# Spreading the first chunk's shares from on-chip memory in two expert layers, and one exponential placed earlier

## The chip, the core and the metric

The kernel runs on one core of a Trainium2 chip. The time is device microseconds of one execution. The engines are TensorE (PE, with its weight loads PEld), VectorE (DVE), ScalarE (ACT), GpSimd (POOL) and SyncE (SP), which here only issues DMAs. Sixteen DMA engines carry the transfers.

## What is computed

Two layers over x of 4 x 256 tokens and 256 channels, all float32. Each layer has a gated attention-like part and an expert part, each with a gate from a bidirectional decaying sum (`_bi_wkv`). The change is in the expert parts alone. Layer 0 has 64 experts of 64 channels, of which 6 are chosen per token, and a shared expert; layer 1 has 8 experts of 256 channels, of which 2 are chosen:

```python
# layer 0
h = relu2(jnp.einsum('th,eih->tei', x, w1))      # relu, squared
h = h * w_dense[:, :, None]                      # share of each expert in each token
routed = jnp.einsum('tei,ehi->th', h, w2)
out = routed + relu2(x @ shared_up.T) @ shared_down.T
# layer 1
top_vals, top_idx = jax.lax.top_k(x_flat @ w_router, 2)
w_tok = zeros.at[rows, top_idx].add(softmax(top_vals))
h = square(relu(einsum('nc,ecd->ned', x_flat, w_fc)))
out = einsum('nec,ne->nc', einsum('ned,edc->nec', h, w_proj), w_tok)
```

## The kernel before

Tokens (NT = 1024) lie along the free dimension, channels on the 128 partitions. `moe_phase` is an expert layer, called with `which` 0 and 1. The hidden channels of all experts are cut into chunks of 256 (`NW` = 16 in layer 0, 8 in layer 1; layer 0 has one more ahead for the shared expert, `FIRST` = 1). A chunk has four units: two blocks of 128 hidden channels by two halves of 512 tokens, `u` = 0 to 3, the half running fastest. Each unit goes through these steps:

- PE, `first_layer` (L1790): four matmuls into bank `u`.
- ACT, `unit` (L1673, L1675): relu from the bank into `h2` (ffn_relu), then the square in place.
- POOL (L1662): `hw` (ffn_weighted) = `h2` times the tile `wide` (ffn_wide), which holds each expert's share spread over the partitions of its channels.
- PE, `second` (L1812): four matmuls that add the unit to the result.

PE runs two chunks ahead with its first step: in `turn` each unit's four L1812 matmuls are followed by four L1790 of the chunk after the next. Before the turns PE has done the L1790 of chunks 0 and 1, so it then stands until POOL has weighted the first unit of chunk 0.

The shares are made by DVE from the router's logits (L1718 to L1771), transposed by PE (L1861) and copied by ACT to `wT` (ffn_weights_t, L1701): one expert per partition, 64 partitions in layer 0 and 8 in layer 1, with 1024 tokens of 4 bytes in a row. SP waits for both halves (`wT_ready`), stores `wT` to a DRAM tensor (ffn_shares, L1638), waits for the store, and then calls `follow` for each chunk. `follow` (L1621 to L1633) waits, from chunk 2 on, for POOL to have weighted the chunk before the last, and spreads the rows from DRAM (L1628). In layer 0 a chunk holds four experts: four DMAs, each of one row to 64 partitions, two for each block `t` of 128 channels; POOL waits for block 0's two before unit 0 and for block 1's two before unit 2. In layer 1 a chunk lies within one expert: one DMA of one row to 128 partitions for all four units. Where `more` is set, `follow` also loads a later chunk's weights (L1605, tile feat); in layer 0 that begins with chunk 1 and the load of chunk 4. After chunk 1 layer 0 also issues the loads of the next part's weights (`ahead_of`, L1899 to L1902). All these DMAs go through SP's one queue, in the order in which they are written.

In layer 1 ACT also computes the exponential for the shares (L1696). It waits for `sub_ready` from DVE and stands behind the relu and square of units 0 and 1; DVE waits for it before L1764.

Of the kernel before, what the change touches and what calls it, by code (L numbers as in the profile page):

```python
# [14 lines left out]
P = 128  # L15
B, T, C = 4, 256, 256
CT = C // P
NT = B * T
# [36 lines left out]
def halves(h):  # L55
    return slice(h * HALF, (h + 1) * HALF)
# [1471 lines left out]
def moe_phase(nc, ctx, a, env, which, prior):  # L1528
# [14 lines left out]
    def sb(n, shape, dt=F32):  # L1543
        return ctx.enter_context(nc.sbuf_tensor(name + n, shape, dt))

    def named(n):
        return sem(name + n)

    UNITS, LEAD, SLOTS = 4, 2, 4
    FIRST, NW = NS // 2, NM // 2  # L1550
# [3 lines left out]
    BLOCKS, ROWS = (2, P // PER) if PER < P else (1, 1)  # L1554
# [10 lines left out]
    wide = sb("wide", [P, 2, BLOCKS, NT])  # L1565
    h2, hw = (sb(n, [P, 2, UNITS, HALF]) for n in ("relu2", "weighted"))
# [7 lines left out]
    wT = sb("weights_t", [E, NT])  # L1574
# [9 lines left out]
    wide_in = [[named(f"wide_in{slot}{t}") for t in range(BLOCKS)] for slot in range(2)]  # L1584
# [16 lines left out]
    def known(c):  # L1601
        return isinstance(c, int)

    def load(sp, n, slot):
        sp.dma_start(chunk[:, slot, :, :],  # L1605
                     a[pre + "chunks"][ds(n, 1), :, :, :].rearrange("o p k n -> (o p) k n")).then_inc(chunk_in[slot], 16)
# [13 lines left out]
    def sync(sp, ahead_of=None):  # L1620
        def follow(c, slot, more):  # L1621

            if not known(c) or c >= 2:
                sp.wait_ge(weighted, (c - 1) * UNITS)
            for t in range(BLOCKS):
                for i in range(ROWS):
                    part = slice(i * P // ROWS, (i + 1) * P // ROWS)
                    sp.dma_start(wide[part, slot % 2, t, :],  # L1628
                                 w_dram[ds((c * BLOCKS + t) * ROWS + i, 1), :].rearrange("o n -> (o n)")
                                 .partition_broadcast(P // ROWS)).then_inc(wide_in[slot % 2][t], 16)  # L1630
            if more:
                sp.wait_ge(chunk_done, c - 1 + FIRST)
                load(sp, c + 2 + FIRST, (slot + 2 + FIRST) % SLOTS)  # L1633

        if late:
            late["sync"](sp)
        sp.wait_ge(wT_ready, NH)
        sp.dma_start(w_dram, wT[:]).then_inc(wT_out, 16)  # L1638
        sp.wait_ge(wT_out, 16)
        for c in range(2):  # L1640
            follow(c, c, c + 2 + FIRST >= SLOTS)
        if which == 0:
            ahead_of(sp)
        with sp.Fori(0, (NW - 4) // 4) as k:
            for j in range(2, 6):
                follow(k * 4 + j, j, True)
        for c in range(NW - 2, NW):
            follow(c, c, False)
# [20 lines left out]
    def scalar(act):  # L1669
        def unit(n, j, u, to):  # L1670

            act.wait_ge(hidden_full, n + 1)
            act.activation(h2[:, j, u, :], banks[u][:], ACT.Relu).then_inc(relu_done, 1)  # L1673
            act.wait_ge(relu_done, n + 1)
            act.activation(to[:, j, u, :], h2[:, j, u, :], ACT.Square).then_inc(square_done, 1)  # L1675

        def units(c, j, first=0):
            for u in range(first, UNITS):
                unit(SHARED + c * UNITS + u, j, u, h2)

        if which == 0:
            unit(0, 1, 0, hw)
            act.wait_ge(logits_full, 1)
            act.activation(sc[:], banks[LOGITS][:, 0:TT * E].rearrange("p (t e) -> p t e", t=TT), ACT.Sigmoid)\
               .then_inc(scores_ready, 1)
            for u in range(1, UNITS):
                unit(u, 1, u, hw)
            late["scalar"](act)
            for u in range(UNITS - 1):
                unit(SHARED + u, 0, u, h2)  # L1690
        else:
            act.preload_act_table_set("natural_log_exp_and_others")
            for u in range(2):
                unit(u, 0, u, h2)
            act.wait_ge(sub_ready, 1)
            act.activation(sc[:], sb_[:], ACT.Exp).then_inc(scores_ready, 1)  # L1696
            for u in range(2, UNITS):
                unit(u, 0, u, h2)
        for h in range(NH):
            act.wait_ge(wT_full, h + 1)  # L1700
            act.activation(wT[:, halves(h)], banks[TURNED[h]][0:E, :], ACT.Copy).then_inc(wT_ready, 1)  # L1701
        if which == 0:
            units(0, 0, UNITS - 1)
        units(1, 1)
        if late:
            late["exp"](act, 0)
        with act.Fori(1, NW // 2) as k:
            units(k * 2, 0)
            if late:
                late["exp"](act, k)  # L1710
            units(k * 2 + 1, 1)
# [95 lines left out]
    def tensor(pe):  # L1807
# [66 lines left out]
        for j in range(SLOTS):  # L1874
            turn(NW // SLOTS - 1, j, ahead=j < SLOTS - LEAD, ends=j == SLOTS - 1)

    return dict(sync=sync, tensor=tensor, scalar=scalar, vector=vector, gpsimd=gpsimd, last_sum=last_sum,
                open_sync=open_sync, open_tensor=open_tensor, start=start)

# [278 lines left out]
```

## Time and profile before

| | us |
|---|---|
| median of 3 runs | 1457.3 |
| lowest, highest | 1453.5, 1460.3 |
| profiled execution | 1452.3 |
| its span, first to last instruction | 1450.5 |
| PE busy | 1365.4 (94%) |
| DVE, ACT, POOL busy | 1079.7, 853.9, 462.1 |

Layer 0's expert part runs from about 1018 to 1259 us of the span, that of layer 1 from about 1330 to the end. The profile is of one execution, and every time of day in the rows counts from the span's start. In a timeline, the bracket at the end of a row is the idle time before it and what ended it; rows of the same kind in a row are merged, with their count. The last matmul of a merged row is modelled a little long (1.88 us for four that follow each other every 1.72 us), so distances are better taken from start to start.

### The profile page before, as it was taken

To read this page: it belongs to the slowest core of one execution; us is meant where nothing else is said; L and a number is where in the kernel's file an instruction comes from. 1 tells how busy PE (TensorE), PEld (TensorE's weight loads), DVE (VectorE), ACT (ScalarE), POOL (GpSimd) and SP (SyncE) were. 2 spreads that over 40 slices of the span, in tenths; PEclk is the share of its full clock that TensorE was granted. 3 is DMA by queue.
4 is the path that set the end of the run, shared out by engine and by line. 5 is a ranking of instruction groups with operands and counts; after the bars stand their busy time and mean duration, and the time that the engine had idled before them with its cause. 6 is when DMAs were issued, how large, how long until landed. Compare 5 with 4: busy or idle time off the path is not lost.

```text
span 1450.5 us, 22073 instructions
## 1 busy us (share of the span) xinstructions
PE 1365.4 (94%) x7888; PEld 767.7 (53%) x7888; DVE 1079.7 (74%) x2468; ACT 853.9 (59%) x1745; POOL 462.1 (32%) x375
## 2 busy tenths in 40 slices
PE   0879999999999999999999999988999999999998
PEld 0534754754664574575475476475444444444443
DVE  8898899889789889989988988955599675613000
ACT  4577677678578667767767857755533333212432
POOL 5151161161153135116116115215064343200432
PEclk9999999999999999999999999979999999999999
DMA  3120030030021022003003002102283444100220
GB/s 108 43 94 16 16 124 9 8 116 22 17 76 62 17 66 73 16 16 123 16 2 124 15 17 77 33 17 94 69 232 101 117 128 117 59 0 0 78 97 29
DMA packets 39092, 88.70 MB, mean 61 GB/s; under 512 B 5384, under 2 KB 25352, under 8 KB 37840
## 3 DMA queue, kind: packets, MB, share of 16 engines
q1 hardware_dynamic: 38704, 87.23, 19.5%
q8 instruction: 62, 1.02, 0.3%
q14 instruction: 38, 0.31, 0.1%
q10 hardware_dynamic: 288, 0.14, 0.0%
HBM read 84.77 MB, written 2.59 MB: 60 GB/s over the span
## 4 chain that ended last, share of the span: by engine, by line
PE 68%; DVE 18%; ACT 8%; issue 3%; DMA 2%; POOL 1%; DVEq 0%; ACTq 0%; SPq 0%; POOLq 0%
PE bank L512 13%; PE bank L1812 12%; PE bank L1790 11%; PE bank L1911 5%; DVE m L1179 5%; PE bank L611 4%; PE bank L626 4%; DVE m L1183 3%; PE bank L574 3%; PE bank L541 3%; DVE conv L1082 3%; PE bank L606 2%; PE bank L617 2%; PE bank L628 2%; ACT conv L834 2%
## 5 line engine op out<-in xcount | busy, mean ns | idle before, releaser
L1082 DVE SCALAR_TENSOR_TENSOR conv<-bank,taps,conv 128x510 f32<-128x510 f32 x366 | 270.4, 743 | 27.7 <-ACT conv L820 18.4
L512 PE MATMUL bank<-rT,wf 128*128 128x512 f32 x512 | 253.8, 611 | 6.9 <-DVE conv L1093 4.1
L1662 POOL TENSOR_TENSOR ffn_weighted<-ffn_relu,ffn_wide 128x512 f32<-128x512 f32 x96 | 128.7, 1374 | 299.9 <-DMA ffn_wide<-ffn_shares 148.0
L1812 PE MATMUL bank<-ffn_weighted,feat 128*128 128x512 f32 x400 | 186.8, 595 | 3.8 <-POOL ffn_weighted L1662 3.8
L1790 PE MATMUL bank<-rT,feat 128*128 128x512 f32 x400 | 187.4, 595 | 0.0
L1325 POOL TENSOR_TENSOR sq<-sq,qsq 128x512 f32<-128x512 f32 x64 | 82.9, 1296 | 270.3 <-ACT sq L1008 269.6
L1673 ACT ACTIVATE ffn_relu<-bank 128x512 f32<-128x512 f32 x100 | 59.6, 596 | 182.3 <-PE bank L1790 182.3
L512 PEld LDWEIGHTS bank<-rT,wf 128*128 128x128 f32 x512 | 89.5, 191 | 87.9 <-issue 73.7
L1812 PEld LDWEIGHTS bank<-ffn_weighted,feat 128*128 128x128 f32 x400 | 76.0, 190 | 100.1 <-issue 98.2
L1790 PEld LDWEIGHTS bank<-rT,feat 128*128 128x128 f32 x400 | 76.0, 191 | 93.9 <-issue 93.1
L574 PE MATMUL bank<-rT,wz 128*128 128x512 f32 x256 | 115.3, 604 | 8.9 <-DVE m L1183 6.1
L549 PE MATMUL bank<-zs,wo 128*128 128x512 f32 x256 | 119.9, 595 | 3.0 <-DVE m L1183 3.0
L820 ACT ACTIVATE conv<-bank,taps 128x512 f32<-128x512 f32 x122 | 84.1, 712 | 47.2 <-PE bank L512 46.7
L1427 DVE TENSOR_TENSOR xT<-xT,bank 128x512 f32<-128x512 f32 x16 | 10.6, 685 | 130.4 <-PE bank L1812 112.7
L1330 POOL TENSOR_TENSOR zs<-zs,rs 128x512 f32<-128x512 f32 x64 | 81.7, 1277 | 62.4 <-DVE rs L1119 61.7
L1372 POOL COPY t<-tmp 32x1024 f32<-32x1024 f32 x16 | 16.5, 1030 | 265.3 <-DVE tmp L1239 264.8
L1209 DVE TENSOR_TENSOR tmp<-mt,rs 128x126 f32<-128x126 f32 (+35 forms) x488 | 99.3, 243 | 1.2 <-DVE mt L1200 0.5
L1343 POOL TENSOR_TENSOR z<-z,mask 128x512 f32<-128x512 f32 x64 | 81.1, 1277 | 43.0 <-DMA z<-decay_rows 41.3
L1179 DVE SCALAR_TENSOR_TENSOR m<-bank,ccol,z 128x512 f32<-128x512 f32 x128 | 94.6, 739 | 0.2
L574 PEld LDWEIGHTS bank<-rT,wz 128*128 128x128 f32 x256 | 48.7, 193 | 74.0 <-issue 62.7
L626 PE MATMUL bank<-m,z 128*128 128x256 f32 x256 | 77.8, 386 | 2.6 <-DVE rs L1119 2.5
L865 ACT ACTIVATE z<-z,gcol 128x256 f32<-128x256 f32 x128 | 63.4, 495 | 23.4 <-POOL z L1343 23.2
(235 smaller groups left out, 2612.0 us busy)
## 6 DMA issues: line engine op xcount, KB each, us to landing
z<-decay_rows SPq DMA_DIRECT2D x64, 384.0 KB, 4.0
ffn_wide<-ffn_shares SPq DMA_DIRECT2D x64, 256.0 KB, 5.3
feat<-in_L_chunks_dram SPq DMA_DIRECT2D x25, 512.0 KB, 4.2
wf<-in_wf_dram SPq DMA_DIRECT2D x8, 1024.0 KB, 4.9
wz<-in_wz_dram SPq DMA_DIRECT2D x8, 512.0 KB, 3.6
wo<-in_wo_dram SPq DMA_DIRECT2D x8, 512.0 KB, 3.8
ffn_wide<-ffn_shares SPq DMA_DIRECT2D x8, 512.0 KB, 4.0
m<-in_fT_dram SPq DMA_DIRECT2D x2, 512.0 KB, 5.1
```

The costliest lines, as they stand in the source:

```text
L512: ins = pe.matmul(banks[bank_of(p, n)][:], wf[:, c, ORDER[n // NH], :], rT[:, c, halves(n % NH)], start=(c == 0), stop=(c == CT - 1))
L549: ins = pe.matmul(banks[b][:], wo[:, v, c * P:(c + 1) * P], zs[:, v, halves(h)], start=(v == 0), stop=(v == GV - 1))
L574: last = pe.matmul(banks[n % 4][:], wz[:, c, v, :], rT[:, c, halves(h)], start=(c == 0), stop=(c == CT - 1))
L626: pe.matmul(b[:, i * T:(i + 1) * T], z[:, v, 2 * s, :], m[:, v * B + s, 0:T], start=True, stop=False, skip_group_check=True)
L820: act.activation(conv[:, n % HF, :], banks[bank_of(p, n)][:], ACT.Copy, scale=taps[:, ORDER[n // NH], KS - 1:KS]).then_inc(conv0_ready, 1)
L1082: dve.scalar_tensor_tensor(acc[:, :, k:], src[:, :, 0:T - k], taps[:, ORDER[n // NH], KS - 1 - k:KS - k], acc[:, :, k:], ALU.mult, ALU.add ...
L1179: dve.scalar_tensor_tensor(to[:, 0:2 * T].rearrange("p (a i) -> p a i", a=2), banks[b0][:].rearrange("p (a i) -> p a i", a=2), ccol[:, v, ...
L1209: return t, dve.tensor_tensor(t, mt[:, j, rows].unsqueeze(2).to_broadcast([P, n, j + 1]), inv[:, j, 0:j + 1].unsqueeze(1).to_broadcast([P, ...
L1325: pool.tensor_tensor(out, out, qsq[:, n // 4, halves(n % NH)], ALU.add).then_inc(sum_ready, 1)
L1662: pool.tensor_tensor(hw[:, j, u, :], h2[:, j, u, :], wide[:, j, u // NH % BLOCKS, halves(u % NH)], ALU.mult).then_inc(weighted, 1)
L1790: last = pe.matmul(banks[u][:], chunk[:, slot, c, t * P:(t + 1) * P], rT[:, c, halves(h)], start=(c == 0), stop=(c == CT - 1))
L1812: last = pe.matmul(banks[4 + 2 * c + h][:], chunk[:, slot, CT + t, c * P:(c + 1) * P], of, start=start, stop=stop, skip_group_check=True)
```

## The change

For chunk 0 alone, `follow` takes the row from `wT` in SBUF and not from the DRAM tensor, and SP issues these DMAs ahead of the store of `wT` and of its wait. Chunk 1 and all later ones still read DRAM; their first issue stands behind the store's wait as before. In layer 1 the exponential of ACT stands ahead of the relu and square of unit 1.

```diff
@@ follow, in sync
                 for i in range(ROWS):
                     part = slice(i * P // ROWS, (i + 1) * P // ROWS)
+                    if known(c) and c == 0:
+                        row = t * ROWS + i
+                        sp.dma_start(wide[part, slot % 2, t, :], wT[row:row + 1, :].unsqueeze(1).to_broadcast([1, P // ROWS, NT]))\
+                          .then_inc(wide_in[slot % 2][t], 16)
+                        continue
                     sp.dma_start(wide[part, slot % 2, t, :],
                                  w_dram[ds((c * BLOCKS + t) * ROWS + i, 1), :].rearrange("o n -> (o n)")
                                  .partition_broadcast(P // ROWS)).then_inc(wide_in[slot % 2][t], 16)
@@ sync
         sp.wait_ge(wT_ready, NH)
+        follow(0, 0, 2 + FIRST >= SLOTS)
         sp.dma_start(w_dram, wT[:]).then_inc(wT_out, 16)
         sp.wait_ge(wT_out, 16)
-        for c in range(2):
-            follow(c, c, c + 2 + FIRST >= SLOTS)
+        follow(1, 1, 3 + FIRST >= SLOTS)
@@ scalar, layer 1
-            for u in range(2):
-                unit(u, 0, u, h2)
+            unit(0, 0, 0, h2)
             act.wait_ge(sub_ready, 1)
             act.activation(sc[:], sb_[:], ACT.Exp).then_inc(scores_ready, 1)
-            for u in range(2, UNITS):
+            for u in range(1, UNITS):
                 unit(u, 0, u, h2)
```

SP's queue in layer 0, from the transposed shares to the mixer's first weights. First before, then after (a name on the left of the arrow is written, those on the right are read; ffn0_shares is the DRAM tensor, ffn0_weights_t the tile `wT`):

```order
76 L1638 DMA ffn0_shares<-ffn0_weights_t 64x1024
77 L1628 DMA ffn0_wide<-ffn0_shares 64x1024 x8
78 L1605 DMA feat<-in_L0_chunks_dram 128x1024
79 L1899 DMA mixer_win<-in_mixer_in_dram 128x2x1024
80 L1900 DMA mixer_wconv<-in_mixer_conv_dram 128x4x512
```

```order
76 L1630 DMA ffn0_wide<-ffn0_weights_t 64x1x1024 x4
77 L1644 DMA ffn0_shares<-ffn0_weights_t 64x1024
78 L1633 DMA ffn0_wide<-ffn0_shares 64x1024 x4
79 L1605 DMA feat<-in_L0_chunks_dram 128x1024
80 L1903 DMA mixer_win<-in_mixer_in_dram 128x2x1024
```

Four of the eight spreads have moved ahead of the store and read ffn0_weights_t; everything else keeps its place. (The line numbers of the changed kernel are higher by 4 or more.) In layer 1 the same happens to the first of its spreads.

ScalarE's order in layer 1, from unit 0's relu (ffn1_relu2 is `h2`, ffn1_scores takes the exponential). Before, then after:

```order
1005 L1673 ACTIVATE ffn1_relu2<-bank 128x512
1006 L1675 ACTIVATE ffn1_relu2<-ffn1_relu2 128x512
1007 L1673 ACTIVATE ffn1_relu2<-bank 128x512
1008 L1675 ACTIVATE ffn1_relu2<-ffn1_relu2 128x512
1009 L1696 ACTIVATE ffn1_scores<-ffn1_biased 128x64
```

```order
1005 L1678 ACTIVATE ffn1_relu2<-bank 128x512
1006 L1680 ACTIVATE ffn1_relu2<-ffn1_relu2 128x512
1007 L1700 ACTIVATE ffn1_scores<-ffn1_biased 128x64
1008 L1678 ACTIVATE ffn1_relu2<-bank 128x512
1009 L1680 ACTIVATE ffn1_relu2<-ffn1_relu2 128x512
```

The exponential has moved ahead of unit 1's two steps.

## Rows read from the trace of the kernel before

**Rows 1.** The page: span, and the busy time of TensorE.

```profile
span 1450.5 us, 22073 instructions
...
PE 1365.4 (94%) x7888; PEld 767.7 (53%) x7888; DVE 1079.7 (74%) x2468; ACT 853.9 (59%) x1745; POOL 462.1 (32%) x375
```

**Rows 2.** The chain that ended last, layer 0: start us, us, what.

```profile
1042.18 0.97 ACT ffn_weights_t L1701 x2
...
1043.17 2.98 DMA ffn_shares<-ffn_weights_t
...
1046.74 4.08 DMA ffn_wide<-ffn_shares
```

**Rows 3.** The same chain, layer 1.

```profile
1343.00 1.78 DMA ffn_shares<-ffn_weights_t
...
1344.80 3.92 DMA ffn_wide<-ffn_shares
```

**Rows 4.** Timeline of PE, layer 0: start us, us, engine, line, instruction.

```profile
1041.67 8.75 PE L1790 MATMUL bank<-rT,feat 128*128 128x512 f32 x20
...
1052.36 2.90 PE L1812 MATMUL bank<-ffn_weighted,feat 128*128 128x512 f32 x4 [1.94 <-POOL ffn_weighted L1662]
1055.06 2.67 PE L1790 MATMUL bank<-rT,feat 128*128 128x512 f32 x4
1057.56 1.88 PE L1812 MATMUL bank<-ffn_weighted,feat 128*128 128x512 f32 x4
...
1061.00 1.88 PE L1812 MATMUL bank<-ffn_weighted,feat 128*128 128x512 f32 x4
```

**Rows 5.** Timeline of PE, layer 1.

```profile
1340.52 1.04 PE L1861 MATMUL bank<-ident,ffn_weights 128*8 128x128 f32 x8
...
1350.26 1.96 PE L1812 MATMUL bank<-ffn_weighted,feat 128*128 128x512 f32 x4 [1.83 <-POOL ffn_weighted L1662]
1352.05 1.88 PE L1790 MATMUL bank<-rT,feat 128*128 128x512 f32 x4
```

**Rows 6.** Stretches; last three columns: granted clock, share of 16 DMA engines, GB/s.

```profile
1446.40:1447.20 0.80, 0.23 (x1) 0.00 (x0) 0.53 (x1) 0.00 (x0) 0.00 (x0) 1.00 0.88 330
1346.50:1348.50 2.00, 1.92 (x5) 0.57 (x3) 0.00 (x0) 1.27 (x3) 0.00 (x0) 1.00 0.80 299
1044.30:1045.80 1.50, 1.50 (x5) 0.71 (x4) 0.00 (x0) 1.04 (x2) 0.00 (x0) 1.00 0.81 175
65.40:66.30 0.90, 0.90 (x10) 0.90 (x10) 0.86 (x2) 0.00 (x0) 0.00 (x0) 1.00 0.85 179
1343.70:1344.40 0.70, 0.70 (x4) 0.22 (x3) 0.00 (x0) 0.67 (x2) 0.00 (x0) 1.00 0.33 47
1048.00:1052.00 4.00, 2.42 (x6) 0.76 (x4) 0.00 (x0) 3.02 (x6) 1.05 (x1) 1.00 1.03 245
...
1052.00:1056.00 4.00, 3.64 (x6) 1.57 (x7) 3.45 (x3) 0.45 (x1) 4.00 (x4) 0.65 1.05 238
```

**Rows 7.** Timeline of POOL, the first units of layer 0 and of layer 1.

```profile
1050.95 12.01 POOL L1662 TENSOR_TENSOR ffn_weighted<-ffn_relu,ffn_wide 128x512 f32<-128x512 f32 x8 [43.26 <-DMA ffn_wide<-ffn_shares]
...
1348.85 9.84 POOL L1662 TENSOR_TENSOR ffn_weighted<-ffn_relu,ffn_wide 128x512 f32<-128x512 f32 x8 [98.44 <-DMA ffn_wide<-ffn_shares]
```

**Rows 8.** Timeline of PE at its first work in the span.

```profile
37.33 3.65 PE L295 MATMUL bank<-pT,rT 128*128 128x64 f32 x16 [37.33 <-DVE rT L238]
40.77 4.70 PE L512 MATMUL bank<-rT,wf 128*128 128x512 f32 x8
...
49.38 1.89 PE L295 MATMUL bank<-pT,rT 128*128 128x64 f32 x16
```

**Rows 9.** Timeline of SP's queue, layer 0.

```profile
1043.17 0.55 SPq L1638 DMA_DIRECT2D ffn_shares<-ffn_weights_t  x1
1046.17 5.00 SPq L1628 DMA_DIRECT2D ffn_wide<-ffn_shares  x8
1051.21 0.58 SPq L1605 DMA_DIRECT2D feat<-in_L_chunks_dram  x1
```

**Rows 10.** Timeline of ACT and DVE in layer 1, around the exponential.

```profile
1336.73 0.23 DVE L1755 TENSOR_TENSOR ffn_biased<-ffn_masked,ffn_top 128x64 f32<-128x64 f32 x1
...
1337.28 0.60 ACT L1673 ACTIVATE ffn_relu<-bank 128x512 f32<-128x512 f32 x1 [2.24 <-PE bank L1790]
...
1338.45 0.24 ACT L1696 ACTIVATE ffn_scores<-ffn_biased 128x64 f32<-128x64 f32 x1
...
1338.80 0.23 DVE L1764 SCALAR_TENSOR_TENSOR ffn_weights<-ffn_marked,ffn_scores 128x64 f32<-128x64 f32 x1 [0.41 <-ACT ffn_scores L1696]
...
1339.55 0.23 DVE L1771 TENSOR_TENSOR ffn_weights<-ffn_weights,ffn_total 128x64 f32<-128x64 f32 x1
```

**Rows 11.** DMAs from issue to landing (last column): the page, then 1065 to 1070 us.

```profile
feat<-in_L_chunks_dram SPq DMA_DIRECT2D x25, 512.0 KB, 4.2
...
feat<-in_L_chunks_dram SPq DMA_DIRECT2D x1, 512.0 KB, 7.2
```

## The prediction

> **What bounds the kernel now.** The page says that TensorE (PE) is busy for 94% of the span, so time is won or lost only where PE stands still [rows 1]. The change lies in the two expert layers, so I read the chain that ended last around the start of each. In both it leaves PE at the same place: two matmul groups end, ScalarE copies the transposed shares to SBUF, SP stores them to DRAM, SP spreads the first chunk's rows from DRAM over the partitions, GpSimd multiplies, and PE goes on [rows 2, 3]. The store costs 2.98 us in layer 0 and 1.78 us in layer 1; the first spread lands 4.08 and 3.92 us after its issue. PE's own timeline says what of this is seen: PE stands still for 1.94 us before 1052.36 in layer 0 and for 1.83 us before 1350.26 in layer 1 [rows 4, 5]. In layer 0 the two groups behind the gap also take 2.70 and 2.50 us from start to start where the next ones take 1.72, a loss of 1.76 us, and the stretch from 1052 to 1056 shows a granted clock of 0.65, that is a time at 1.2 instead of 2.4 GHz; layer 1 shows no such loss [rows 4 to 6]. All that this change could give back is 1.94 + 1.76 + 1.83 = 5.5 us, 0.38% of the time.
>
> **What it moves on SP.** The first chunk's spreads (four DMAs in layer 0, one in layer 1) now go out when the store did, at 1043.17 and 1343.00, and the store follows them. If a spread from SBUF moved like one from DRAM, everything would be there 3.0 and 1.8 us earlier and both gaps would close. The whole question is how fast 16 DMA engines can read one row: the row of an expert lies in one partition (0 to 3 in layer 0, 0 in layer 1), and it is read 64 times, or 128 times, from there.
>
> **What a DMA from few partitions costs.** No row shows this very transfer, so I bound it by the neighbours. The columns are the share of 16 engines and GB/s; their quotient is the rate of one engine while it is busy [rows 6]. The output store, from 128 partitions: 330/(0.88 x 16) = 23.4 GB/s. A spread to 128 partitions from DRAM: 299/(0.80 x 16) = 23.4. The store of the shares in layer 0, from 64 partitions: 175/(0.81 x 16) = 13.5. The store of the decay rows, from 32 partitions: 179/(0.85 x 16) = 13.2. The store of the shares in layer 1, from 8 partitions: 47/(0.33 x 16) = 8.9. Two stores that both end in DRAM differ by 1.7, so DRAM's side isn't what halves the rate; where fewer partitions are read, an engine gets less. The spreads of layer 0 show the same on the writing side, 245/(1.03 x 16) = 14.9 with 64 partitions each against 23.4 with 128. I read this as paths into SBUF that engines share, two to a path where half the partitions take part, each path passing 2 x 13.5 = 27.0 GB/s. One partition then has one path, whatever the number of engines. I take 27.0 GB/s, since it is the rate of a path that is shared, as it would be here; 23.4, that of one engine alone on it, is the slow bound; the other bound is that there is no such limit and the spreads gain 5.5 us (first rival).
>
> The Trainium skill has a rule that speaks against this change: SBUF — State Buffer, section "Door 1: The DMA port swizzle (why `[64,N]` ≈ `[32,N]`)", says that partitions 0 to 3 all lie on one of sixteen ports, and that a transfer over them reached 27.6 GB/s. By that figure the transfers below would take 38.0 and 19.0 us instead of 38.8 and 19.4 us, and the sum would be an estimated 1.2 us smaller. The stores from 64 and from 32 partitions agree with its claim that these two are alike (13.5 and 13.2 GB/s).
>
> **Layer 0.** A chunk is four DMAs of 64 x 4096 B, 1.049 MB in all, so 38.8 us at 27.0 GB/s, and 19.4 us for the first two. The store took 2.98 us, of which 1.2 us is its movement (0.262 MB at 216 GB/s), so 1.8 us stand beside the movement. First half lands at 1043.17 + 1.8 + 19.4 = 1064.4, all four at 1083.8. From landing to GpSimd's start it was 0.13 us (1050.82 to 1050.95 [rows 2, 7]), from there to PE 1.41 us. (Layer 1: 0.12 and 1.41 [rows 3, 5, 7].) Units 0 and 1 need the first half: PE starts again at 1065.9 instead of 1052.36 and runs out at about 1075 (two units of 3.44 us, plus a slow restart). Unit 2 needs the second half: PE starts it at 1083.8 + 1.54 = 1085.3 instead of 1061.00 [rows 4]. That is **+24.3 us**, and it contains the gain of the store's 3.0 us. A second restart comes on top. Its nearest rows are at the span's start, where PE comes from 37 us of rest: 16 small matmuls take 3.65 us against 1.89 us later, 8 large ones 4.70 us against 2 x 1.88 [rows 4, 8], a loss of 2.7 us. The near bound is layer 1's gap, with none. I take **+2.7**, the rest being nearer to the long one.
>
> What comes behind: the store is issued at about 1045.7 but queues behind the spreads and lands near 1085.0. Only then does SP issue chunk 1's spreads, the weight load of chunk 4 and the mixer's weights; eight spreads took 5.00 us to issue, so four take 2.5 [rows 9]. Chunk 1's first half lands near 1091; PE wants it at 1085.3 + 2 x 3.44 + 2.7 = 1094.9, GpSimd 1.4 us earlier. That leaves some 2 us. The load of chunk 4, issued at 1088 and wanted by PE at 1094.9, has 7 us; one such load took 4.2 us in the median and 7.2 us where it followed four spreads [rows 11]. I count 0, with 0 to 3 as bounds.
>
> **Layer 1.** One DMA of 128 x 4096 B from partition 0: 0.524 MB, 19.4 us, landing at 1343.00 + 1.8 + 19.4 = 1364.2; PE starts at 1365.7 instead of 1350.26, **+15.5**, and a slow restart after 17 us of rest, **+2.7**. It feeds all four units, so there is no second wait. Chunk 1's spread is issued about 1 us after that landing and PE has 13.7 us until it needs it.
>
> **The exponential.** In layer 1 it starts at 1338.45, behind unit 1's square; its input is there at 1336.96. Moving it ahead ends VectorE's wait of 0.41 us. Behind that stand the transposes on PE, but PE reaches them at 1340.52 straight out of its own matmuls, 0.74 us after VectorE's last product at 1339.78 [rows 5, 10]. ScalarE's copy then waits for unit 3's relu and square, which PE's end releases. The relu of unit 1 is due at 1337.28 and the exponential takes 0.24 us from about 1337.0. So it is worth **0**, and PE's own matmuls are what covers it.
>
> **Sum.** 24.3 + 2.7 + 15.5 + 2.7 = 45.2 us. The profiled execution took 1452.3 us (span 1450.5, 1.8 around it), so 1497.5 on its scale. The median of the three runs is 1457.3, 5 us above it, so I forecast **1502.5 us** for a median.
>
> **Rivals.** *No shared path (not slower).* Sixteen engines read one row as fast as they read 128 partitions. Then GpSimd starts 3.0 us earlier in layer 0, at 1047.95, and its product is there at 1049.4, before PE's last matmul of that run ends at 1050.42; in layer 1 1.8 of the 1.83 us go. Gain 5.5 us, 1451.8. It decides from the point where the first half lands by 1048.9, which asks for over 130 GB/s out of one partition pair; the rows with 8 partitions speak against it. Also possible is part of it, a path limit of 40 to 60 GB/s, with some 10 to 30 us lost, 1467 to 1487.
> *A single partition is slower than a path.* All rows have at least 8 partitions. At half the rate (13.5 GB/s) the halves land at 1083.8 and 1122.6 and layer 1 at 1383.6: 24.3 + 38.8 + 15.5 + 19.4 + 5.4 = 103 us, 1561.
> *Engines, not paths.* A DMA whose source is one partition might be given to a single engine. At 23.4 GB/s that engine needs 1.049/23.4 = 44.8 us and 22.4 us: 9.0 us more than the sum, 1511. The time hardly tells it apart, the records do: packets of 0.17 us on one engine rather than some 2.4 us on sixteen.
> The Trainium skill, DMA: Bandwidth & Descriptors, section "Why a DMA increments its semaphore by 16 and not by 1", has the slowest dimension that isn't 1 choose the number of engines, and that is 64 or 128 here. By that page the DMA spreads over sixteen engines.
>
> **Chances.** Serial reading at 23 to 28 GB/s, by paths or by one engine: 0.79. Half of that rate: 0.06. Part of the limit: 0.05. No limit: 0.10. Within the first, the bounds are 45.2 - 5.4 (no slow restarts) = 40 us and 45.2 + 9.0 + 3 = 57 us, so 1497 to 1514; three runs of the kernel before spread over 7 us, which makes it 1493 to 1518, and I reach a little into the partial case: 1484 to 1522. A measurement of this kernel can tell about 0.5% from no change. Slower by more than that: 0.89, within it: 0.09, faster: 0.02, since even the full gain is 0.38%.
>
> **What would show it.** GpSimd's first product at about 1064.5 and 1364.3 instead of 1050.95 and 1348.85, its third at about 1084; PE idle for some 15, 10 and 17 us; a DMA share near 1 at some 27 GB/s while the spreads run; SP's store issued by 1046 and landing after 1084. Wrong would be a first product before 1055, GB/s in the hundreds in these stretches, or a wait on chunk 4's weights of over 3 us.

## The result, and the profile after

The changed kernel takes 1496.7 us (median of 6 runs, 1496.2 to 1503.4) against 1458.2 us (6 runs): 1.028 times the time of before, interval 1.026 to 1.031. It is slower, by 38.5 us between the medians. The profiled execution took 1496.4 us with a span of 1494.6, 44.1 us more than the profiled one of before.

TensorE's timeline has the loss in three gaps. Columns: start, duration, engine, line, instruction, and in brackets the idle time before it and what ended it. Layer 0, to be read against [rows 4]:

```profile
1041.07 8.75 PE L1794 MATMUL bank<-rT,feat 128*128 128x512 f32 x20
1065.58 3.75 PE L1816 MATMUL bank<-ffn_weighted,feat 128*128 128x512 f32 x4 [15.76 <-POOL ffn_weighted L1667]
...
1084.23 3.78 PE L1816 MATMUL bank<-ffn_weighted,feat 128*128 128x512 f32 x4 [9.65 <-POOL ffn_weighted L1667]
1087.81 2.92 PE L1794 MATMUL bank<-rT,feat 128*128 128x512 f32 x4
1090.56 1.88 PE L1816 MATMUL bank<-ffn_weighted,feat 128*128 128x512 f32 x4
```

Layer 1, against [rows 5]:

```profile
1391.68 3.75 PE L1816 MATMUL bank<-ffn_weighted,feat 128*128 128x512 f32 x4 [17.12 <-POOL ffn_weighted L1667]
1395.22 2.81 PE L1794 MATMUL bank<-rT,feat 128*128 128x512 f32 x4
1397.87 1.88 PE L1816 MATMUL bank<-ffn_weighted,feat 128*128 128x512 f32 x4
```

The gaps of 1.94 and 1.83 us have become 15.76 + 9.65 and 17.12 us. Who was late says POOL's timeline, against [rows 7]: it waited for the spreads, twice in layer 0, since units 0 and 1 need two of them and unit 2 the other two.

```profile
1064.17 2.94 POOL L1667 TENSOR_TENSOR ffn_weighted<-ffn_relu,ffn_wide 128x512 f32<-128x512 f32 x2 [57.11 <-DMA ffn_wide<-ffn_weights_t]
1082.91 2.48 POOL L1667 TENSOR_TENSOR ffn_weighted<-ffn_relu,ffn_wide 128x512 f32<-128x512 f32 x2 [15.80 <-DMA ffn_wide<-ffn_weights_t]
...
1390.27 9.82 POOL L1667 TENSOR_TENSOR ffn_weighted<-ffn_relu,ffn_wide 128x512 f32<-128x512 f32 x8 [113.73 <-DMA ffn_wide<-ffn_weights_t]
```

What the DMA engines did meanwhile, by stretches as in [rows 6] (last three columns: granted clock, share of 16 engines, GB/s), and the landings (last column: median us from issue):

```profile
1045.00:1055.00 10.00, 4.82 (x12) 1.84 (x10) 3.05 (x6) 5.36 (x9) 0.00 (x0) 0.87 0.91 26
1370.00:1388.00 18.00, 4.56 (x11) 1.71 (x9) 0.00 (x0) 4.37 (x8) 0.00 (x0) 0.68 0.99 29
```

```profile
ffn_wide<-ffn_weights_t SPq DMA_DIRECT2D x4, 256.0 KB, 25.4
ffn_wide<-ffn_weights_t SPq DMA_DIRECT2D x1, 512.0 KB, 21.0
```

Nearly all sixteen engines are busy, and together they move 26 to 29 GB/s, where spreads from DRAM moved 245 and 299. So they are occupied without moving much. Whether they stand in one line for one path, as I had forecast, is what the probes below test.

SP's queue shows the one thing that came out differently, against [rows 9]:

```profile
1042.56 17.47 SPq L1630 DMA_DIRECT2D ffn_wide<-ffn_weights_t  x4
1060.07 9.59 SPq L1644 DMA_DIRECT2D ffn_shares<-ffn_weights_t  x1
1083.94 2.42 SPq L1633 DMA_DIRECT2D ffn_wide<-ffn_shares  x4
```

Issuing four DMAs took 17.5 us instead of 2.5, and the store behind them 9.6 us. One by one, the first two took 0.54 and 0.60 us, the third 6.61 and the fourth 9.59. In layer 1, where a single spread stands ahead of the store, SP issued both in 0.53 us each (1369.14 and 1369.72), though that spread was as slow.

### The profile page after: what moved, and what is told of

Same layout as the page of the kernel before. It is cut to its first block, busy times and chain, and to the rows that moved or that the text cites. A ratio compares the mean times of both kernels' runs of the same rounds, so it can differ in the third digit from the quotient of the medians.

```text
span 1494.6 us, 22073 instructions
## 1 busy us (share of the span) xinstructions
PE 1371.6 (92%) x7888; PEld 769.9 (52%) x7888; DVE 1069.2 (72%) x2468; ACT 856.1 (57%) x1745; POOL 459.2 (31%) x375
## 4 chain that ended last, share of the span: by engine, by line
PE 66%; DVE 18%; ACT 7%; issue 4%; DMA 3%; POOL 1%; DVEq 0%; ACTq 0%; SPq 0%; POOLq 0%
PE bank L512 13%; PE bank L1816 11%; PE bank L1794 10%; DVE m L1179 5%; PE bank L1915 5%; PE bank L611 4%; PE bank L626 3%; DVE m L1183 3%; PE bank L574 3%; DMA ffn_wide<-ffn_weights_t 3%; PE bank L541 3%; DVE conv L1082 3%; PE bank L606 2%; PE bank L617 2%; ACT conv L834 2%
## 5 line engine op out<-in xcount | busy, mean ns | idle before, releaser
L1082 DVE SCALAR_TENSOR_TENSOR conv<-bank,taps,conv 128x510 f32<-128x510 f32 x366 | 270.5, 743 | 27.7 <-ACT conv L820 18.3
L1816 PE MATMUL bank<-ffn_weighted,feat 128*128 128x512 f32 x400 | 191.3, 607 | 42.5 <-POOL ffn_weighted L1667 42.5
L1209 DVE TENSOR_TENSOR tmp<-mt,rs 128x126 f32<-128x126 f32 (+35 forms) x488 | 102.7, 257 | 1.2 <-DVE mt L1200 0.5
```

The lines of the kernel that those rows point to most:

```text
L1082: dve.scalar_tensor_tensor(acc[:, :, k:], src[:, :, 0:T - k], taps[:, ORDER[n // NH], KS - 1 - k:KS - k], acc[:, :, k:], ALU.mult, ALU.add ...
L1209: return t, dve.tensor_tensor(t, mt[:, j, rows].unsqueeze(2).to_broadcast([P, n, j + 1]), inv[:, j, 0:j + 1].unsqueeze(1).to_broadcast([P, ...
L1816: last = pe.matmul(banks[4 + 2 * c + h][:], chunk[:, slot, CT + t, c * P:(c + 1) * P], of, start=start, stop=stop, skip_group_check=True)
```

## Experiments

"The changed kernel" is the one above; ratios are to the kernel before, measured on the same chip.

### One row, many rows, and pairs of rows

```python
one(0, 64)     # rows[0:1, :] repeated to 64 partitions; then to 128, then to the upper 64
rows[0:64, :]  # 64 partitions to 64; then 128 to 128, 32 to 32
# then pairs of one(0, 64) from SP and one(r, 64) from ACT, with r = 1, 32, 64, 4
```

> Only transfers, nothing of the reference is computed. One row of 4096 B is copied inside SBUF: from partition 0 to 64 partitions, to 128, and to the upper 64; then 64, 32 and 128 partitions each to itself elsewhere; then one DRAM row to 64 and to 128 partitions; then four pairs of one-row copies at the same time from two queues, where the second row lies in partition 1, 32, 64 or 4 beside partition 0. My theory (a path into SBUF of some 27 GB/s that several partitions share): one row to 64 lands after 1.8 + 9.5 = 11 us, to 128 after 21 us; 64 partitions to 64 after 3.0 us, 128 to 128 after 3.5 us; in the pairs with partitions 1 and 32 both need 20 us, with 64 and 4 both are done after 11 us. Rival 1 (a single partition is the limit, not a path): all four pairs are done after 11 us. Rival 2 (a row read over and over is slow for each engine, wherever it lies): all four pairs need 20 us. Rival 3 (any DMA from SBUF to SBUF is slow): 64 to 64 needs 11 us too.

Measured, from issue to landing (last column; to_one is the single row, to_all many rows, to_dram one row out of DRAM):

```profile
to_one<-rows SPq DMA_DIRECT2D x1, 512.0 KB, 20.7
to_all<-rows SPq DMA_DIRECT2D x1, 512.0 KB, 2.9
to_dram<-rows_dram SPq DMA_DIRECT2D x1, 512.0 KB, 3.4
...
to_one<-rows SPq DMA_DIRECT2D x1, 256.0 KB, 11.1
to_all<-rows SPq DMA_DIRECT2D x1, 256.0 KB, 2.9
```

The same bytes, the same number of partitions written, the same queue: 20.7 us out of one partition, 2.9 us out of 128, 3.4 us out of one row of DRAM. So neither SBUF to SBUF (rival 3) nor the repetition as such is slow; a repeated row out of DRAM took 0.5 us more than 128 rows out of SBUF. The first two cases came in as expected to within 0.3 us. The pairs were a poor design. In all four one copy landed long before the other:

```profile
to_same_port<-rows ACTq DMA_DIRECT2D x1, 256.0 KB, 20.7
to_same_port<-rows SPq DMA_DIRECT2D x1, 256.0 KB, 11.8
...
to_other_port<-rows SPq DMA_DIRECT2D x1, 256.0 KB, 11.0
to_other_port<-rows ACTq DMA_DIRECT2D x1, 256.0 KB, 18.3
```

In each, one queue's copy landed after 11 to 12 us, nearly as if alone, and the other's 7 to 9 us later. I read this as one copy after the other, the engines mostly on one row and then on the next. Two copies in turn need some 20 us by the theory and by rivals 1 and 2 alike, so the pairs say little. They were not quite alike: with partition 1 or 32 beside 0 the later copy needed 20.7 us, with 64 or 4 it needed 18.7 and 18.3, and over the first 9 us the pairs moved 27 and 31 GB/s. That goes the way of the theory, but it is far smaller than the 20 against 11 us that I had asked for.

### Sets of partitions

```python
src = rows[lo:hi:by, :]      # n partitions (rows[lo:hi, :] where by is 1), each row read eight times, into DRAM
sp.dma_start(to[name], src.unsqueeze(1).to_broadcast([n, 8, NT]))
```

> Only transfers, nothing of the reference is computed. In the first probe the paired copies went one after the other, so it couldn't tell a shared path from a row that is slow for every engine. Here one DMA at a time reads n partitions, each row of 4096 B eight times, into DRAM. An engine reads one partition's row, and the sets differ in which partitions they hold: 0,1,2,3; 0,4,8,12; 0,32,64,96; 0 to 7; 0,4,..,28; 0 to 15; 0,4,..,60; 0,8,..,120; and last partition 0 alone. The Trainium skill (SBUF — State Buffer, section Door 1) maps partitions to ports by groups of four, with p and p+32 on one port. By that map and 27 GB/s a port, 0-1-2-3 needs 131 kB over one port, 4.9 us, and 0-4-8-12 over four ports 1.3 us; 0-32-64-96 over two ports 2.5 us; 0 to 7 over two ports 9.8 us; 0,4,..,28 over eight ports 1.3 us; 0 to 15 over four ports 5.0 us, 0,4,..,60 and 0,8,..,120 over eight ports 2.5 us; each plus 1.8 us beside the movement. Shared path (my theory, without saying which partitions share): sets with the same number of partitions differ strongly. Rival 1 (the single partition is the limit): each engine has a partition of its own, so all sets move at an engine's full rate, 1.3 us. Rival 2 (a row that is read again and again is slow wherever it lies): all sets of four are equally slow.

One stretch inside each case's movement, in the order of the expectation without the last (columns: stretch, length, POOL busy, clock, share of 16 engines, GB/s):

```profile
6.20:10.80 4.60, 0.00 (x0) 1.00 0.21 23
12.90:14.10 1.20, 0.00 (x0) 1.00 0.14 58
15.80:18.10 2.30, 0.00 (x0) 1.00 0.20 41
20.20:24.80 4.60, 0.00 (x0) 1.00 0.41 45
26.90:28.00 1.10, 0.00 (x0) 1.00 0.29 119
29.80:34.60 4.80, 0.00 (x0) 1.00 0.83 90
36.60:39.00 2.40, 0.00 (x0) 1.00 0.67 149
40.80:43.20 2.40, 0.00 (x0) 1.00 0.70 149
```

GB/s over (share x 16) is the rate of one busy engine:

| partitions read | GB/s of one engine | engines to a port, by the map |
|---|---|---|
| 0, 1, 2, 3 | 6.8 | 4 |
| 0, 4, 8, 12 | 25.9 | 1 |
| 0, 32, 64, 96 | 12.8 | 2 |
| 0 to 7 | 6.9 | 4 |
| 0, 4, .., 28 | 25.6 | 1 |
| 0 to 15 | 6.8 | 4 |
| 0, 4, .., 60 | 13.9 | 2 |
| 0, 8, .., 120 | 13.3 | 2 |

The rate follows the last column alone, at about 27 GB/s for a port, whatever the number of partitions or the number of engines. Rival 1 (each partition has its own 27 GB/s) asked for 26 in every row; rival 2 (a repeated row is slow) asked for the same low rate in the first three. Both fall. (The last case, partition 0 alone, holds 32 KB, too little for a rate that means much; between 44.5 and 45.8 it moved 25 GB/s.) The port map of the Trainium skill (SBUF — State Buffer, "Door 1") agrees with every row, including 0, 32, 64, 96, where it puts p and p + 32 on one port. One number of my expectation was a slip: 262 kB over two ports is 4.9 us and not 9.8; the row's 6.9 GB/s is what two ports give.

### The same place in the queue, many partitions

```diff
-sp.dma_start(wide[part, slot % 2, t, :], wT[row:row + 1, :].unsqueeze(1).to_broadcast([1, P // ROWS, NT]))
+sp.dma_start(wide[part, slot % 2, t, :], wT[:] if which == 0 else rT[:, 0, :])
 # ... .then_inc as before
```

> The changed kernel, but the first chunk's spreads read as many partitions as they write: the 64 rows of the transposed shares in layer 0, and 128 partitions of another tile in layer 1. So the first chunk is weighted with wrong shares; bytes, queue places, waits and everything else are those of the change. Theory (shared paths into the partitions that are read): the first half lands 3 to 4.5 us after 1042.6, TensorE's gaps of 15.8, 9.7 and 17.1 us are gone, and the time falls below the kernel before by up to 5.5 us: ratio 0.996 to 1.000, 45 us less than the changed kernel. Rival (reading from SBUF ahead of the store costs it by queue order or by SBUF-to-SBUF as such): it stays near the changed kernel, ratio 1.02 to 1.03.

Ratio 0.994 (0.993 to 0.996), 1447.5 us. TensorE's timeline has no idle time left ahead of the weighted matmuls, in layer 0 (at 1049.89) or in layer 1 (at 1344.02):

```profile
1041.30 8.75 PE L1794 MATMUL bank<-rT,feat 128*128 128x512 f32 x20
1049.89 1.88 PE L1816 MATMUL bank<-ffn_weighted,feat 128*128 128x512 f32 x4
1051.60 1.88 PE L1794 MATMUL bank<-rT,feat 128*128 128x512 f32 x4
...
1337.15 7.03 PE L1794 MATMUL bank<-rT,feat 128*128 128x512 f32 x16
1344.02 1.88 PE L1816 MATMUL bank<-ffn_weighted,feat 128*128 128x512 f32 x4
```

The order, the waits and the bytes are those of the change; only the source differs (many rows once each in place of one row repeated, so the shares of chunk 0 are not the right ones). With that the kernel is 49 us faster than the changed one, and SP issues its four DMAs in 3.2 us. This is the first rival of the prediction, built on purpose. It gains more than I had put as its ceiling: 10 us between the medians, 6.3 us between the profiled executions (1452.3 and 1446.0), against 5.5. The ratio also lies below the 0.996 to 1.000 that I had expected.

### Layer 1 alone, and the exponential alone

```diff
 # layer 1 alone: in layer 0 the store and its wait stand first again
-                    if known(c) and c == 0:
+                    if which == 1 and known(c) and c == 0:
 # ...
-        follow(0, 0, 2 + FIRST >= SLOTS)
+        if which == 1:
+            follow(0, 0, 2 + FIRST >= SLOTS)
         sp.dma_start(w_dram, wT[:]).then_inc(wT_out, 16)
         sp.wait_ge(wT_out, 16)
+        if which == 0:
+            follow(0, 0, 2 + FIRST >= SLOTS)
```

> The change without its part in layer 0: there the store and the spreads from DRAM stand as before. Theory: the losses of the two layers are separate and add up. Layer 1 cost 15.3 us of waiting and 2.75 us of slow restart, so 18.0 us over the kernel before, ratio 1.0125. Rival: the delay in layer 0 shifts something that layer 1 needs (or the other way), and layer 1 alone costs clearly less than 16 or more than 20 us.

Ratio 1.012 (1.010 to 1.014), 1474.6 us, so 17.2 us over before, of 38.5 for both. The wait in layer 1 is the same as in the changed kernel, the slow stretch behind it is not:

```profile
1371.13 3.57 PE L1819 MATMUL bank<-ffn_weighted,feat 128*128 128x512 f32 x4 [17.15 <-POOL ffn_weighted L1670]
1374.54 1.88 PE L1797 MATMUL bank<-rT,feat 128*128 128x512 f32 x4
1376.25 1.88 PE L1819 MATMUL bank<-ffn_weighted,feat 128*128 128x512 f32 x4
```

The two groups take 3.41 and 1.71 us from start to start, a loss of 1.7 us, where the changed kernel lost 2.75 behind a gap of the same length. The 17.2 us lie within the 16 to 20 that separate layers asked for. Layer 0 alone was not run, so that the layers add up rests on the profile: the changed kernel's layer 0 costs 23.8 + 2.9 us and its layer 1 15.3 + 2.7, and these make the 44.1 us between the spans to within 0.6.

```diff
 # the exponential alone, in the kernel before
-            for u in range(2):
-                unit(u, 0, u, h2)
+            unit(0, 0, 0, h2)
             act.wait_ge(sub_ready, 1)
             act.activation(sc[:], sb_[:], ACT.Exp).then_inc(scores_ready, 1)
-            for u in range(2, UNITS):
+            for u in range(1, UNITS):
```

> The kernel before with the exponential of layer 1 ahead of unit 1's relu, and nothing else. Theory: 0 us, ratio 0.998 to 1.002; VectorE's wait of 0.41 us before its first product with the scores goes, its last product ends 0.3 to 0.4 us earlier, and TensorE's transposes still start straight out of its own matmuls. Rival: the exponential delays unit 1's relu or the transposes follow it, and the gap of 1.83 us before layer 1's first weighted matmul changes by over 0.2 us.

Ratio 0.999 (0.996 to 1.001), 1454.2 us: no change that can be measured. VectorE's product with the scores has no wait before it any more, its last one ends 1.1 us before the transposes (0.74 before), and the transposes still start where TensorE's own matmuls end:

```profile
1342.25 0.23 DVE L1763 SCALAR_TENSOR_TENSOR ffn_weights<-ffn_marked,ffn_scores 128x64 f32<-128x64 f32 x1
...
1343.00 0.23 DVE L1770 TENSOR_TENSOR ffn_weights<-ffn_weights,ffn_total 128x64 f32<-128x64 f32 x1
...
1344.34 1.04 PE L1860 MATMUL bank<-ident,ffn_weights 128*8 128x128 f32 x8
...
1354.19 3.03 PE L1811 MATMUL bank<-ffn_weighted,feat 128*128 128x512 f32 x4 [1.95 <-POOL ffn_weighted L1662]
1357.02 2.54 PE L1789 MATMUL bank<-rT,feat 128*128 128x512 f32 x4
```

The last two rows tell something else. Behind the gap of layer 1, which is hardly longer than before (1.95 against 1.83 us), the two groups take 2.83 and 2.38 us from start to start instead of 1.79 and 1.72, 1.7 us lost, which the profile of before did not have there [rows 5].

### Shortening the gap: few rows first, or TensorE as the spreader

The kernel before pays for a store of all rows and a wait. Chunk 0 needs only 4 rows of 64, or 1 of 8.

```diff
-        sp.dma_start(w_dram, wT[:]).then_inc(wT_out, 16)
-        sp.wait_ge(wT_out, 16)
-        for c in range(2):
-            follow(c, c, c + 2 + FIRST >= SLOTS)
+        now = BLOCKS * ROWS
+        sp.dma_start(w_dram[0:now, :], wT[0:now, :]).then_inc(wT_out, 16)
+        sp.wait_ge(wT_out, 16)
+        follow(0, 0, 2 + FIRST >= SLOTS)
+        sp.dma_start(w_dram[now:, :], wT[now:, :]).then_inc(wT_out, 16)
+        sp.wait_ge(wT_out, 32)
+        follow(1, 1, 3 + FIRST >= SLOTS)
```

> The kernel before, but SP first stores only the rows that chunk 0 needs (4 in layer 0, 1 in layer 1), waits, spreads them from DRAM, and stores the rest behind. Theory: the store's landing falls from 2.98 us to about 1.8 us in layer 0 (the time that 8 rows took in layer 1) and stays 1.7 to 1.8 us in layer 1. TensorE's gap in layer 0 shrinks by 1.2 us, and part of the 1.8 to 2.9 us lost to the lower clock behind it may go; 1.2 to 3 us in all, ratio 0.998 to 0.999 against a resolution of some 0.2%. Rival (the store's time is nearly all latency): the gap stays within 0.3 us.

Ratio 0.995 (0.993 to 0.997), 1448.9 us: faster than both kernels by more than the noise, and more than the 0.998 to 0.999 that I had expected. The waits behind the small stores are 1.76 and 1.24 us (SP goes on at 1044.92 and 1341.43), the gaps shrink to 0.82 and 1.03 us, and no slow group follows either of them:

```profile
1043.16 0.34 SPq L1639 DMA_DIRECT2D ffn_shares<-ffn_weights_t  x1
1044.92 2.46 SPq L1628 DMA_DIRECT2D ffn_wide<-ffn_shares  x4
...
1051.24 1.95 PE L1815 MATMUL bank<-ffn_weighted,feat 128*128 128x512 f32 x4 [0.82 <-POOL ffn_weighted L1665]
1053.03 1.88 PE L1793 MATMUL bank<-rT,feat 128*128 128x512 f32 x4
...
1340.19 0.26 SPq L1639 DMA_DIRECT2D ffn_shares<-ffn_weights_t  x1
1341.43 0.32 SPq L1628 DMA_DIRECT2D ffn_wide<-ffn_shares  x1
...
1346.64 1.96 PE L1815 MATMUL bank<-ffn_weighted,feat 128*128 128x512 f32 x4 [1.03 <-POOL ffn_weighted L1665]
```

Between the profiled executions: 1.12 + 1.76 us in layer 0 and 0.80 us in layer 1, 3.7 us, and the spans differ by 3.6 (1450.5 and 1446.9). The medians differ by 9.0. In layer 1 I had expected no gain; a store of one row landed 0.5 us sooner than one of eight.

The other way has no transfer at all for the first two units (for layer 1: for all four). Before its transposes TensorE multiplies one expert's column, repeated as stationary operand, by the identity:

```python
col = w[:, h * TT // NH + t, i:i + 1].to_broadcast([P, P // ROWS])
last = pe.matmul(banks[SPREAD[h]][i * P // ROWS:(i + 1) * P // ROWS, t * P:(t + 1) * P], col, ident[:], start=True, stop=True)
# ScalarE then copies the bank to wide[:, 0, 0, half]
```

> The kernel before, but TensorE spreads the shares that the first two units need: matmuls whose stationary operand is one expert's column of shares, repeated, against the identity, and ScalarE copies the bank to the wide tile; no DMA for them. 16 more small matmuls in layer 0 and 8 in layer 1 (0.13 us each: 2.1 and 1.05 us), 4 more copies of 0.52 us on ScalarE. Theory: both gaps of TensorE before the first weighted matmul vanish (1.94 and 1.83 us, and the clock's loss of 1.8 to 2.9 us behind the first), against 2.1 + 1.05 us of matmuls and some 0.6 us that TensorE waits for ScalarE's copy of the transposed shares in layer 0. Net 2 to 4 us faster than before, more if the gaps also cost clock in the usual run: ratio 0.994 to 0.999. Rival: the added work sits on the same chain and costs what it gives, ratio 0.999 to 1.002.

Ratio 0.996 (0.995 to 0.998), 1450.9 us. Both gaps are gone, but not for nothing. Layer 0 waits 0.72 us for ScalarE's copy of the transposed shares, and the spreading matmuls take more than the transposes do, 1.79 us from start to start for the eight of layer 1 (0.22 us each, where a transpose takes 0.11 from start to start; the trace has two records for each spreading matmul, hence x16):

```profile
1347.47 1.95 PE L1878 MATMUL bank<-ident,ffn_weights 128*128 128x128 f32 x16
1349.26 1.04 PE L1886 MATMUL bank<-ident,ffn_weights 128*8 128x128 f32 x8
```

In layer 1 they cost what the gap did (1.79 against 1.83 us). In layer 0 they take 1.90 us, with the wait 2.62, against a gap of 1.94 us and slow groups of 1.76. That leaves about 1 us of gain, and the medians show 7.0. The profile can't say where the rest comes from: its execution took 1458.95 us, the longest of the ten, and was late before it reached the edit.

> Layer 0 as in the kernel that stores four rows first, layer 1 as in the one where TensorE spreads. Theory: gains 1.2 to 3 us in layer 0 and 0.8 us or more in layer 1; gap of layer 1 gone, that of layer 0 at 0.7 us. Ratio 0.996 to 0.999. If gaps of TensorE in the usual run cost more clock than in the profiled one, as the kernel with many source rows suggests (10 us under the median where the profile gave 6), the kernel without any gap (TensorE's spread in both layers) is the faster of the two.

The mixture (few rows first in layer 0, TensorE in layer 1) has 0.997 (0.995 to 0.998), 1450.3 us. Its gap in layer 0 is 0.82 us (0.7 expected), and in layer 1 there is none. The three intervals overlap, so the order among them stays open; the simplest has the lowest median. That the kernel without any gap would be the fastest, as I had thought possible, isn't borne out.

## Why the prediction held

The forecast was 1502.5 us in a range of 1484 to 1522; the time is 1496.7. Against the profiled execution, which the sum was made for, it was 1497.5 and became 1496.4. Step by step:

- *The rate.* 27.0 GB/s out of one partition, from the store of 64 partitions (2 x 13.5): measured 26 to 29. The first half landed 21.5 us after the first issue (1042.56 to 1064.05) where 21.2 was the sum, the product of unit 0 was started at 1064.17 (forecast 1064.5), unit 2's at 1082.91 (1084). The number was right, the way to it only in part. I had two engines share a path because half the partitions take part; then 32 partitions should have given half of 13.5, and they gave 13.2. The sets 0, 4, .., 28 and 0, 4, .., 60 show why: with the partitions from 32 on added, each engine got half (13.9 after 25.6 GB/s), so these share the ports of the first 32. Of the 8.9 for 8 partitions I made nothing; 0 to 7 measured 6.9 in the probe.
- *Layer 0.* From the first issue to TensorE's unit 2 it is now 1084.23 - 1042.56 = 41.7 us, before 1061.00 - 1043.17 = 17.8: +23.8, forecast +24.3.
- *Layer 1.* 1391.68 - 1369.14 = 22.5 against 7.3 us: +15.3, forecast +15.5.
- *Slow restarts.* The two groups behind the last gap take 3.58 + 2.75 us in layer 0 and 3.54 + 2.65 in layer 1 instead of 2 x 1.72, so 2.9 and 2.75 us; forecast 2.7 each, from the restart at the span's start. The granted clock over these groups was 0.55 and 0.56, near the lower of its two levels. That both came so close is in part luck: behind the first gap of layer 0 (15.76 us, clock 0.65) the loss was 2.0 us, and with layer 1 alone it was 1.7 behind 17.15 us.
- *The exponential.* 0. The run with it alone shows no change outside its interval, and in its profile the transposes start where they should.
- *What comes behind.* No wait on chunk 1 or on chunk 4's weights, as counted; but the step to it was wrong. I had SP issue the store by 1046; it went out at 1060 to 1070, because SP was held while it issued the spreads. It cost nothing that can be seen: SP went on to chunk 1 at 1083.94, where I had the store land near 1085.0, and no gap follows in TensorE's timeline.
- *One engine or a port.* The share of sixteen engines near 1 at 26 to 29 GB/s excludes the single engine, and the sets of partitions show that engines share a port.

Two sizes were off. The median of before stood 5 us over its profiled execution, and I added these 5 us to the changed kernel, which doesn't have them: its median is its profiled time. That is nearly all of the 6 us between forecast and result. A part of what lifts the usual run of before can be seen in other profiles. In layer 1 the four matmuls between the two halves of the router, ahead of what the edits touch there, took 1.96 us in the profiles of before, after, many rows, few rows first and TensorE as the spreader. With the exponential alone they took 3.26 us, with layer 1 alone 2.68, and in the mixture 3.42:

```profile
1331.18 3.42 PE L1811 MATMUL bank<-rT,feat 128*128 128x512 f32 x4
```

Up to that place the kernel with the exponential alone is the kernel before, so such stretches come and go from run to run. Why five of six runs of the changed kernel lie within 2 us, and those of before spread over 14, isn't settled.

The other is the ceiling of a kernel without gaps, which I gave as 5.5 us, 0.38%, and from which I drew that "faster" was nearly excluded. The profile of before happened to have no slow groups behind layer 1's gap; the profile with the exponential alone has them, 1.7 us. The four versions with these gaps shortened or removed gained 0.3 to 0.6% between medians. How much of that the gaps account for isn't shown. With few rows first the profiles and the waits in them say 3.6 us and the lowest runs 4.6 (1451.2 and 1446.6), the medians 9.0; and the exponential alone, which removes no gap, has a median 3.2 us lower too. What the runs do show is that the time goes with the mean granted clock: of the 35 runs of before beside the experiments, the 13 below 1456 us have 0.988 to 0.992, the 22 above it 0.985 to 0.988, and few rows first has 0.991 to 0.993 in seven of its eight. Had the spread been quick, the change would have been faster by just about what can be measured, not "within".

## What to carry to other kernels

Before a DMA is turned from DRAM to SBUF as its source to save a round trip, count from how many ports it reads: a row repeated out of one partition moved at some 27 GB/s though sixteen engines took part, and 0.5 MB of it took 21 us, while DRAM gave the same row in 3.4 us. If a store must land before it is read back, send the few rows that are needed first and the rest behind. And a gap of 2 us in TensorE may cost nearly twice its length, once as waiting and once as clock (1.94 + 1.76 us in layer 0), so closing a short one is worth a try where its length alone would not be.

## What was not expected of the hardware

- Sixteen DMA engines read one row side by side and moved 26 to 29 GB/s in sum, the rate of a port in the probe, with 0.91 to 0.99 of them counted as busy. A busy share says nothing of bytes moved.
- Slow transfers can hold the queue that issues: four DMAs took 17.5 us to issue instead of 2.5, nearly all of it at the third and fourth; a single one took 0.53 us. Something urgent behind the four on the same queue would have been stuck.
- Two one-row copies on two queues, started within 0.1 us of each other, landed after 11 to 12 and after 18 to 21 us, so they ran mostly one after the other.
- A store of four rows let SP go on after 1.76 us, one of a single row after 1.24 us, one of 8 rows after 1.78 us and one of 64 rows after 2.98 us.
- TensorE's groups behind gaps of 0.82 and 1.03 us ran at full pace; behind gaps of 1.94, 1.95, 2.25 and 2.34 us (kernel before, layer 1 alone, and both layers with the exponential alone) they lost 1.7 to 1.8 us, behind one of 1.83 us (layer 1 of the kernel before) nothing. Long gaps did not cost much more: 2.0, 2.9 and 2.75 us behind 15.76, 9.65 and 17.12 us, and 1.7 behind 17.15.
